# A two-layer gated cross-attention and expert kernel: how the second attention opens, with two batches of x projected in a row, keys between by-query units, and unread products in TensorE's waits

## What is computed

```python
x = x + tanh(g_xattn[0]) * attention0(norm(x), ctx, ctx)     # softmax over the query axis
x = x + tanh(g_ffn[0])   * experts0(norm(x))                 # 8 experts, the top 2 of them
x = x + tanh(g_xattn[1]) * attention1(norm(x), ctx)          # this change
x = x + tanh(g_ffn[1])   * experts1(norm(x))                 # 15 experts, top 3, and a shared one

# attention1
q, k, v    = split(norm(x) @ Wqkv + bqkv)
_, ka, va  = split(ctx @ Wqkv_aux + bqkv_aux)
p, pa      = softmax(q @ k.T * scale), softmax(q @ ka.T * scale)     # two softmaxes for each query
out        = ((p @ v) * (1 - gate) + (pa @ va) * gate) @ Wo + bo
```

## Time and profile before

| | |
|---|---|
| median of 3 executions | 1251.21 us (1250.08 to 1251.69) |
| the profiled execution | 1247.79 us |
| its span, first to last instruction | 1245.7 us |
| TensorE busy | 1172.0 us, 94% |
| VectorE, ScalarE, GpSimd busy | 597.1, 477.6, 390.7 us |
| mean granted TensorE clock | 0.970 |

### The profile page before, as it was taken

How to read it: one execution, slowest core, us unless ns; L and a number is a source line. 1 busy time by engine, 2 the same in 40 slices (tenths; PEclk the granted TensorE clock), 3 DMA queues, 4 the chain that set the end, 5 groups by cost and what they waited for, 6 DMA issues and landing times. The chain is left out here.

```text
span 1245.7 us, 29066 instructions
## 1 busy us (share of the span) xinstructions
PE 1172.0 (94%) x11367; PEld 901.1 (72%) x11367; DVE 597.1 (48%) x1432; ACT 477.6 (38%) x1130; POOL 390.7 (31%) x410
## 2 busy tenths in 40 slices
PE   6999999978999999977799999999988999999998
PEld 4767777756999999944466666667665579999985
DVE  5777777774211101165556665666656711121126
ACT  3545555522332333222444444444454223323311
POOL 3666666632322221131100110110112145555420
PEclk9999999968999999985899999999999999999999
DMA  6011111306999998540200100100000459999965
GB/s 180 26 34 34 35 34 52 100 14 239 377 328 321 332 326 321 185 138 1 85 14 14 32 20 14 32 8 3 8 9 14 153 173 357 344 359 357 343 222 169
DMA packets 64371, 180.92 MB, mean 145 GB/s; under 512 B 10156, under 2 KB 36588, under 8 KB 55788
## 3 DMA queue, kind: packets, MB, share of 16 engines
q1 hardware_dynamic: 55068, 156.40, 36.6%
q0 software_dynamic: 8064, 22.03, 4.9%
q10 hardware_dynamic: 1104, 0.64, 0.2%
HBM read 163.11 MB, written 15.93 MB: 144 GB/s over the span
## 5 line engine op out<-in xcount | busy, mean ns | idle before, releaser
L2219 ACT ACTIVATE ex_hT<-kept_psum,ex_w 128x128 f32<-128x128 f32 x464 | 132.3, 368 | 294.9 <-PE kept_psum L2274 294.9
L2274 PE MATMUL kept_psum<-ex_xT,ex_w 128*128 128x128 f32 x1856 | 222.6, 276 | 0.0
L2274 PEld LDWEIGHTS kept_psum<-ex_xT,ex_w 128*128 128x128 f32 x1856 | 215.8, 193 | 0.1
L2285 PE MATMUL kept_psum<-ex_w,ex_hT 128*128 128x256 f32 x928 | 213.9, 379 | 0.0
L2181 DVE TENSOR_TENSOR ex_yt<-kept_psum,ex_b 128x256 f32<-128x256 f32 x84 | 35.6, 424 | 353.9 <-PE kept_psum L2285 353.9
L2285 PEld LDWEIGHTS kept_psum<-ex_w,ex_hT 128*128 128x128 f32 x928 | 170.1, 190 | 19.7
L2147 POOL DMA_INDIRECT ex_results<-ex_yt,ex_to_row x84 | 82.8, 985 | 254.7 <-DVE ex_yt L2181 254.7
L1217 ACT ACTIVATE at_probs<-kept_psum 120x800 f32<-120x800 f32 (+2 forms) x128 | 101.1, 841 | 86.3 <-PE kept_psum L1378 86.3
L1067 DVE TENSOR_REDUCE at_negmax<-kept_psum 100x2 f32<-100x722 f32 x128 | 115.2, 900 | 0.0
L568 ACT ACTIVATE at_probs<-kept_psum 120x800 f32<-120x800 f32 (+1 forms) x96 | 80.0, 836 | 74.1 <-PE kept_psum L691 74.0
L410 DVE TENSOR_REDUCE at_negmax<-kept_psum 120x8 bf16<-120x800 f32 (+1 forms) x96 | 90.5, 984 | 24.0 <-PE kept_psum L682 23.6
(11 more groups left out here) (249 smaller groups left out, 1685.0 us busy)
## 6 DMA issues: line engine op xcount, KB each, us to landing
ex_w<-in_pack_in SPq DMA_DIRECT2D x32, 1028.0 KB, 6.0
ex_w<-in_pack_out SPq DMA_DIRECT2D x32, 1024.0 KB, 7.6
ex_w<-in_pack_in SPq DMA_DIRECT2D x52, 514.0 KB, 5.3
ex_w<-in_pack_out SPq DMA_DIRECT2D x52, 512.0 KB, 6.0
at_ctx<-in_ctxT SPq DMA_DIRECT2D x31, 361.0 KB, 3.8
ex_normed<-ex_xhat SPq DMA_DIRECT2D x16, 200.0 KB
ex_ways<-ex_results SPq DMA_DIRECT2D x6, 400.0 KB
ex_w<-ex_results SPq DMA_DIRECT2D x6, 400.0 KB
```

The source lines that it names most:

```text
L2219: last = act.activation(hT[t % N][:, c, :], ps_h[:, (t * U + u) % N, i * P:(i + 1) * P], ACT.Gelu, bias=w1[t % N][:, B1 + c:B1 + c + 1])
L2274: last = pe.matmul(ps_h[:, (t * U + u) % N, i * P:(i + 1) * P], w1[t % N][:, c * ff + f:c * ff + f + P], xT[t % N][:, c, :], start=(c == 0 ...
L2285: last = pe.matmul(ps_y[:, t % N, 0:D], hT[t % N][:, c, :], w2[t % N][:, c * D:(c + 1) * D], start=(c == 0), stop=(c == FC - 1))
```

## The change

It touches the opening of `attend1` and the first of the transfers that feed it.

Step -2 is gone. Ahead of the loop TensorE now turns x of batches 0 and 1 and projects both. The keys of batch 4 are not made ahead but in step -1, one half after the first `by_query` unit and one after the second. In step 0 `by_query` of batch 1 starts ahead of `turn_max` of batch 0. `keep_warm` issues products of the identity with 128 columns of a weight into a bank that is free at that place; nobody reads them. There are 29: 9 ahead of the first transposition, 2 ahead of the first `by_query`, 3 in step -1, and five times 3 in step 0.

The first two transfers of ways are cut in two, batches 0 and 1 first. VectorE adds these, takes moments of two batches, and only then adds the rest; moments, root and newton of the first group of four are done as two groups of two. GpSimd takes the first root ahead of its additions. VectorE's additions of group 2 move from the end of step -1 to the middle of step 0, those of group 3 from the end of step 0 to the end of step 1, and the handover with `prep.load` follows one step later. Moments of the last two groups of four are in steps 2 and 5.

```diff
+    GROUPS = [range(0, 2), range(2, GB)] + [range(g * GB, (g + 1) * GB) for g in range(1, NG)]
+    GROUP_OF = [g for g, bs in enumerate(GROUPS) for b in bs]
     STRIPS, HALVES, PAIRS = 4, 2, 3
     HH, HS = H // HALVES, H // STRIPS
     NC, NK, NX, NQ, NV, PRE = early.NC, early.NK, 3, 3, 3, 2
-    EARLY_KEYS = range(KC * early.AHEAD, KC * NK)
+    KEYED = NK - 1
+    EARLY_KEYS = range(KC * early.AHEAD, KC * KEYED)
+
+    def key_batch(t):
+        b = KEYED if t == -1 else t + NK - 1
+        return b if t and b < B else None
+
+    def x_batch(t):
+        return t + 2 if 0 <= t < B - 2 else None
...
-    STEPS = range(-2, B + 4)
-    ahead = [(n, b) for b in range(PRE) for n in ("value01", "value2")]
-    ring = ahead + [(n, t + off) for t in STEPS for n, off in (LIGHT_ORDER if t in LIGHT else ORDER) if on(t + off) and (n, t + off) not in ahead
-                    and not (n in ("key0", "key1") and t + off < NK) and not (n in ("value01", "value2") and t + off == PRE)]
+    STEPS = range(-1, B + 4)
+
+    def used(n, off, t):
+        b = key_batch(t) if n in ("key0", "key1") else x_batch(t) if n in ("xT", "own") else t + off
+        return b if b is not None and on(b) and not (n in ("value01", "value2") and b <= PRE) else None
+
+    opening = [(n, b) for b in range(PRE) for n in ("value01", "value2")] + [(n, b) for n in ("xT", "own") for b in range(2)]
+    ring = opening + [(n, used(n, off, t)) for t in STEPS for n, off in (LIGHT_ORDER if t in LIGHT else ORDER) if used(n, off, t) is not None]
...
-            if t == 1:
+            if t == 2:
...
+        root(0)
         fed.gpsimd(pool, 0)
-        root(0)
+        root(1)
         for g in range(1, NG):
             fed.gpsimd(pool, g)
         for b in range(B + 4):
-            if b == 1:
+            if b == 2:
...
+        fed.vector_first(dve)
+        moments(0)
         fed.vector(dve, 0)
-        moments(0)
         newton(0)
         normed(0)
         normed(1)
         take_values01(PRE)
         take_value2(PRE)
+        moments(1)
         fed.vector(dve, 1)
...
+            if t == 0:
+                newton(1)
+                normed(2)
             if on(t + 1):
                 maxima(t + 1, 1)
             if on(t - 2):
                 normalize(t - 2, 0)
-            if t == -2:
-                moments(1)
-            if t > 0 and t % GB == 1 and (t + 3) // GB + 1 < NG:
-                moments((t + 3) // GB + 1)
+            if t == 0:
+                fed.vector(dve, 2)
+            if t in (1, 2):
+                moments(t + 1)
+            if t == 5:
+                moments(4)
...
+            if t == 0:
+                normed(3)
+            if t == 1:
+                newton(2)
+                normed(4)
+            if t > 0 and on(t + 4):
                 if (t + 4) % GB == 0:
-                    newton((t + 4) // GB)
+                    newton((t + 4) // GB + 1)
                 normed(t + 4)
...
-            if t in (-1, 0):
-                fed.vector(dve, t + 3)
-            if t == 0:
+            if t == 1:
+                fed.vector(dve, 3)
...
+        take_xT(0)
+        take_xT(1)
+        take_own(0)
         fed.scalar(act, 1)
+        take_own(1)
         for t in STEPS:
-            if t == 2:
+            if t == 3:
                 second.enter(act)
-            if on(t + NK - 1) and t > 0:
...
+        def keep_warm(bank, n):
+            for _ in range(n):
+                pe.matmul(bank[:, 0:P], ident[:, :], wa[:, 0, 0:P], start=True, stop=True)
...
+        keep_warm(psum[:, 2, :], 9)
+        turn_x(0)
+        turn_x(1)
+        pe.wait_ge(w_loaded, 32)
+        project_own(0)
+        project_own(1)
+        keep_warm(psum[:, 2, :], 2)
         for t in STEPS:
-            if t == 2:
+            if t == 3:
                 second.enter(pe)
             if t == -1:
                 pe.wait_ge(filled, 6 + 2 * NV)
                 pe.wait_ge(rest_loaded, 16 * 7)
-            if on(t):
+            if on(t) and t != 0:
                 turn_max(t)
             if on(t + 1):
                 by_query(t + 1, 0)
-            if on(t + NK - 1) and t > 0:
-                project_key(t + NK - 1, 0)
+            if t == 0:
+                turn_max(t)
+            if key_batch(t) is not None:
+                project_key(key_batch(t), 0)
             if t in LIGHT:
                 values01(t + 1)
             if on(t):
                 by_key(t, 0)
             if t in LIGHT:
                 values2(t + 1)
-            if on(t + NK - 1) and t > 0:
-                project_key(t + NK - 1, 1)
+            if key_batch(t) is not None and t != -1:
+                project_key(key_batch(t), 1)
+            if t == 0:
+                keep_warm(into("xT", 2), 3)
             if on(t + 1):
                 by_query(t + 1, 1)
+            if t == -1:
+                project_key(key_batch(t), 1)
...
+            if t == 0:
+                keep_warm(into("xT", 2), 3)
             if on(t):
                 by_key(t, 1)
-            if on(t + 2):
-                turn_x(t + 2)
+            if x_batch(t) is not None:
+                turn_x(x_batch(t))
             if on(t - 1):
                 sum_up(t - 1, 1, range(HG // 2 if t in LIGHT else HG))
+            if t == 0:
+                keep_warm(into("own", 2), 3)
             if on(t + 1):
                 by_query(t + 1, 2)
...
+            if t == -1:
+                keep_warm(into("max", 0), 3)
+            if t == 0:
+                keep_warm(into("value_own", 0), 3)
             if on(t + 1):
                 by_query(t + 1, 3)
+            if t == 0:
+                keep_warm(into("value_own", 0), 3)
...
+        FIRST = 0 if shared else 2
+        first_in = [] if shared else [m.sem(f"first_in{i}") for i in range(top)]
...
+            def load_way(i, j0, j1, loaded):
+                row = i % top * TOK + (i // top * GB + j0) * T
+                sp.dma_start(parts[i][:, j0:j1, :],
+                             ways[row:row + (j1 - j0) * T].rearrange("(b t) d -> t b d", t=T)).then_inc(loaded, 16)
+
+            for i, loaded in enumerate(first_in):
+                load_way(i, 0, FIRST, loaded)
             for i in range(NG * top):
-                g, way = i // top, i % top
-                row = way * TOK + g * GB * T
-                sp.dma_start(parts[i][:, :, :],
-                             ways[row:row + GB * T].rearrange("(b t) d -> t b d", t=T)).then_inc(ways_in[i], 16)
+                load_way(i, FIRST if i < top else 0, GB, ways_in[i])
...
+        def add_first(dve):
+            for i in range(top):
+                dve.wait_ge(first_in[i], 16)
+                need(dve, added, i * FIRST)
+                for b in range(FIRST):
+                    dve.scalar_tensor_tensor(out=xs[:, b, :], in0=parts[i][:, b, :], scalar=gates[:, i, b:b + 1], in1=xs[:, b, :],
+                                             op0=ALU.mult, op1=ALU.add).then_inc(added, 1)
+
         def add_ways(dve, g):
+            j0 = FIRST if g == 0 else 0
             for i in range(g * top, (g + 1) * top):
                 way = i % top
                 dve.wait_ge(ways_in[i], 16)
-                need(dve, added, i * (GB - 1) if way else 0)
-                for j in range(GB - 1):
+                need(dve, added, g * top * (GB - 1) + top * j0 + way * (GB - 1 - j0) if way else 0)
+                for j in range(j0, GB - 1):
```

More of the change, by code:

```diff
@@ L1017, in gpsimd @@
                 if b % GB == 0 and b // GB + 1 < NG:
-                    root(b // GB + 1)
+                    root(b // GB + 2)
             p = pair_at(b + 2)
@@ L1027, in moments @@
         def moments(g):
-            if g < 2:
-                fed.summed(dve, g)
-            for b in range(g * GB, (g + 1) * GB):
+            bs = GROUPS[g]
+            if g == 0:
+                fed.summed_first(dve)
+            elif g < 3:
+                fed.summed(dve, g - 1)
+            for b in bs:
                 last = dve.bn_stats(stats[:, b, :], xs[:, b, :])
@@ L1252, in scalar @@
                 exponents(t, 1)
[L1253 to L1254 removed]
+            if x_batch(t) is not None:
+                take_xT(x_batch(t))
             if on(t - 1):
                 take_sum(t - 1, 1)
[L1257 to L1258 removed]
+            if x_batch(t) is not None and t not in LIGHT:
+                take_own(x_batch(t))
             if B <= t <= B + 1:
                 prep.early_scalar(act, range(t - B, t - B + 1))
[L1261 to L1262 removed]
             if t == -1:
+                fed.scalar(act, 2)
+                fed.scalar(act, 3)
                 second.leave(act)
@@ L1266, in scalar @@
                 exponents(t, 2)
-            if on(t + 2) and t in LIGHT:
-                take_own(t + 2)
+            if x_batch(t) is not None and t in LIGHT:
+                take_own(x_batch(t))
             if t == 3:
@@ L1297, in into @@
                 before, at = ring[n]
```

(10 more changed lines are left out.)

45 lines of the change are left out of this document (21 added, 24 removed).

## The result

The changed kernel takes 1231.49 us, median of six executions (1229.47 to 1233.45), against 1250.64 us (1249.54 to 1251.69) of the kernel before on the same chip: ratio 0.9845, 95% interval 0.9831 to 0.9859. That is 19.2 us less; 16 were forecast (1235 us), and the range of 1230 to 1243 held the time.

What follows compares the result with a forecast made beforehand. It took the second attention's opening as bound by TensorE's waits and reduced clock. The new order's marks sum to 18 us, less 2 for a clock fall: 16 us off the 1251.2 us median gives 1235, range 1230 to 1243.

Steps and rivals of the forecast that it cites:

- Marks 1 to 3: Opening of second attention: first by_query unit 4.1 us earlier, batch 0's last maxima 9.0 us, first by_key 11.7 us.
- Mark 4: End of step 0, before at 599.26: at 581.2 with the clock full, 18 us earlier.
- the clock's share: Between step -1's last unit and first by_key: a clock fall somewhat likelier, costing 1.5 to 3 us, taken as 2.
- Afterwards: Steps after 0: step 1 gains 2 us, additions at step 2's head cost about as much; the rest nothing.
- additions there that hold up by_key: Rival, head of step 2: additions delay by_key, 2 us lost; moves the time inside the range only.
- several falls: Clock at half in several stretches; chance 0.25 together with half the clock until step 0.
- half the clock until step 0: Rival: clock falls at first x, returns only in step 0; gain 7 to 8 us, 1243.5; shared chance 0.25.
- the fall at mark 3 alone: Likeliest case: one clock fall ahead of the first by_key, gain 16 us, 1235 us; chance 0.40.
- Its own sign of being wrong: PEclk 0.50 over most of 550 to 575, by_key queued behind unread products, or later steps over a us longer.
- No fall at the seam: Rival: clock stays full between step -1 and the first by_key; gain 18 us, 1233.2 us; chance 0.27.
- slower: Rival: unread products don't hold the clock and stand in the way in step 0; 1255 us; chance 0.04.
- No effect: Time within 0.2% (1249 to 1254), needing half the clock through step -1 and half of step 0; chance 0.04.

Runs made afterwards that it cites:

- e4: Changed kernel with 12 more unread products between steps -1 and 0 (5 ahead of batch 1's first unit, 7 behind turn_max): 1230.4 us, 0.9827 of the kernel before.
- e7: The changed kernel once more, nothing altered, on the same chip as e8: 1232.97 us, 0.9842 of the kernel before.
- e3: Changed kernel with group 3's six additions between the third and fourth maxima of step 1, not at its end: 1228.1 us, 0.9808 of the kernel before.
- e8: Changed kernel with e3 and e4 together, plus six and four unread products around step 1's last by_query unit: 1225.42 us, 0.9791 of the kernel before.
- e5: e8 with the first two transfers of ways whole again: 1228.9 us, 0.9816 of the kernel before.
- e11: e8 with six unread products instead of three in each of five places of step 0: 1229.1 us, 0.9815 of the kernel before.
- e2: Kernel before with 56 unread products added where TensorE waited, nothing else changed: 1239.3 us, 0.9906 of the kernel before.
- e1: Changed kernel without its 29 unread products: 1237.2 us, 0.9880 of the kernel before.

## Why the prediction was right, and where its sizes were off

**Marks 1 to 3: right.** First transposition at 544.99 (forecast 545.2), first unit 550.06 (550.6), last maxima 560.68 (561.4), first by_key 562.96 (563.7). VectorE bounded step -1 with units 2.4 us apart. With the clock held, the order is worth 7.4 us up to step 1. One by one, 3.9 us are the earlier first x (1.8 of them the halved transfers), batch 1 ahead 0.5, additions off the seam 2.0, the unit ahead of turn_max 0.8. Moments in twos, the root ahead and the place of batch 4's keys were not tried alone.

**Mark 4 and the clock's share: right in kind, priced a little high.** Step 1 was to begin near 583, with one fall at the seam; it began at 581.19 with that fall. The forecast priced the fall at 1.5 to 3 us; it cost 1.3 and 2.2 us. So the opening gained 18.2 us where 16 were forecast. Of the two stretches that it read for this, one kept the clock and one lost it; that a fall was the likelier (0.40 against 0.27) was the author's estimate, and both profiles of the changed kernel have one. `e4` shows that the clock holds when products fill the idleness there, with the same turn_max (0.28 us) between.

**The term that failed is "Afterwards".** It put the additions at the head of step 2 at about what step 1 gains, so nothing in all; steps 1 and 2 together took 4.2 us more than before, and 1.6 us more in `e7`. Step 1 took 21.28 us in `e7` as forecast (22), but 23.83 us with a second fall of the clock. Step 2 took 27.2 us in both profiles, 4.3 us more than before, where 1 to 2 were forecast: the wait of 2.62 us, and in both a stretch at half the clock that began 1.3 to 1.5 us behind it. The forecast had named additions there that hold up by_key as a rival (2 us), and that half of this rival came true. It had weighed falls at the seam only. It wanted at most one stretch at half, and there were three in the first profile (564.0, 598.2 and 611.8) and two in `e7`; that is "several falls", which it gave 0.25 together with half the clock until step 0, and not the fall at mark 3 alone, which it gave 0.40. Its own sign of being wrong, later steps longer by more than a us in all, came true in step 2. `e3` and `e8` show that the wait and the falls can be taken out: the first two steps behind the opening take 44.6 us in `e8`, against 46.8 us before.

**What made up for it is the base, and that was luck.** "I count from the median" took the distance of 3.4 us between profile and median as the same for both kernels. By the profiles the gain is 14.8 us (1247.8 to 1233.0), by the medians 19.2 us. The second profile of the kernel before shows 4.3 us more from S to step 3, 1.5 of them up to the end of the opening, 1.8 in step 1 and 1.0 in step 2, with more time at half the clock. A typical execution before lost more to the clock than the one I read, so there was more to gain. The loss in steps 1 and 2 and this gain have opposite signs, and neither was in the sum.

**Rivals.** No fall at the seam, 18 us: the trace shows a fall. Half the clock until step 0, and slower: PEclk is 1.00 from 545 to 563. No effect: it asked for half the clock through step -1, too. That half transfers land no earlier: `e5` shows 1.8 us.

## What to carry to other kernels

Where TensorE works in bursts between other engines' results, read the granted clock per step before counting waits: with the old order the full clock alone is worth 12 us (56 products that nobody reads), the new order alone 15 us, and both 19 us, since each keeps the clock up in part (0.58 in the opening before, 0.73 with the order alone, 1.00 with the products alone). Size such products by the wait, a little less than it (in `e8` three of them, 0.7 us, left 0.15 to 0.87 us of four waits; in `e11` six in each of the five places cost 1.6 us), and look for the next place where the clock falls once the first is mended: three more places filled or freed brought another 7.5 us. And a kernel whose time hangs on the clock needs more than one profile as a base.

## What was not expected of the hardware

The same program falls to half the clock at different places from one execution to the next. At the waits of 1.74 and 1.39 us in step 1 it fell in the first profile of the changed kernel (behind the first wait, half from 598.1 to 605.0) and in `e4` (in the second), but not in `e7`, nor in the first profile before. A fall came 1.3 to 1.5 us behind the wait of 2.62 us in step 2 in both profiles of the changed kernel, and none behind the same wait in step 1 of `e2`: the clock fell there only at 607.6. Nor did one follow waits of 1.59 and 2.34 us at that place in `e4` and `e1`. A stretch at half lasted 3.4 to 31 us.

In `e8` and the kernels that start from it the trace shows no fall in this stage, but whole times don't settle into one value. Five executions lay within 1 us (`e4`) and 2.6 us (`e8`), against 4.7 us of the changed kernel on the same chip as `e8`, yet within 5.8 us in `e5` on that chip, where the clock of the profile is 1.00 in this stage as in `e8`. So not all of the scatter is shown to be the clock of this stage.
